# A decoder's state space layer: the skip term as a GpSimd product and a VectorE addition, in place of matmuls with a diagonal

## The chip, the cores and the metric

One NeuronCore of one Trainium2 chip runs the whole kernel in one launch. The metric is device time in microseconds (us), the median of several executions. The engines are TensorE (PE in the rows; PEld is its weight load), VectorE (DVE), ScalarE (ACT), GpSimd (POOL) and SyncE (SP), which here only issues transfers.

## What is computed

The kernel is a two-layer decoder on 32 sequences of 64 tokens, width 256: attention, cross attention and routed experts, then a state space layer, cross attention and low-rank experts, each followed by a residual and a layer norm. The change is in the state space layer (`_L1_attn_ref`):

```python
zxbcdt = u @ W_in.T
z, xBC, dt = jnp.split(zxbcdt, [D_INNER, D_INNER + CONV_DIM], axis=-1)
...
xBC = jax.nn.silu(conv)
x, B, C = jnp.split(xBC, [D_XB, 2 * D_XB], axis=-1)
x = jnp.repeat(x.reshape(b, l, XB_GROUPS, D_STATE), REPEAT, axis=2).reshape(b, l, D_INNER)
...
y = Y_diag + Y_off + xc * D[:, None]
...
y = y * jax.nn.silu(z)
yg = y.reshape(b, l, NGROUPS, NORM_GS)
rstd = jax.lax.rsqrt(jnp.mean(yg * yg, axis=-1, keepdims=True) + EPS)
y = (yg * rstd).reshape(b, l, D_INNER) * norm_weight
return y @ W_out.T
```

The skip term is `xc * D`: the convolved and activated input x, 128 channels that are repeated for 4 groups, times one number per head (8 heads of 64 channels, 512 in all).

## The kernel before

The 2048 tokens are 16 tiles of 128 (two sequences of 64) in 4 chunks of 512. The sequences are so short that the state space recurrence is written as one 64x64 matrix of weights per head and sequence, as in attention.

`layer1_state_space` writes out each engine's program by hand, in 16 slots, one per tile, followed by 7 slots that overlap the cross attention. In slot s the engines do, in this order:

- TensorE: `mix(s)` (L2288), which multiplies the inputs by the weights `es` and leaves the tile's output y in PSUM; `products(s + 1)` (L2273), the products of B and C for the next tile; `square_sums(s - 1)` (L2297); `put_out(s - 2)` (L2307), the output projection. Around them lie, by a table of jobs (`dealt`), the input projections of the chunks to come (`fill`, L2242), transposes (L2248, L2254) and the sums of decays (`segments`, L2261).
- VectorE: `weigh(s)` (L2131) finishes the weights, for which mix(s) waits; `add_up(s - 3)` (L2151, four instructions) adds the projected output to the residual; `gated(s)` (L2142) takes y out of PSUM with the gate silu(z); `statistics(s - 3)` (L2162, L2164) for the layer norm; a convolution (L2113, three instructions); `mean_square(s - 1)` (L2170); often a second convolution; `time(s + 1)` (L2124).
- ScalarE: exponentials of the decays (`decay`, L2030), evacuation of the projections (`evacuate`, L2000 to L2016), squares of the gated output (L2036), activation of the convolved rows (L2024), the layer norm (L2040).
- GpSimd: decay products for later tiles (`decay_steps`, L1922, two in each of slots 0 and 1 of every four), a weight product for tile s + 3 (`weight_steps`, L1928), `rms_power(s - 1)` (L1935), which waits for mean_square(s - 1), and `variance_power(s - 3)` (L1942 to L1948).

The skip term is made by TensorE. Ahead of the slots GpSimd forms `ddiag` (L1958), for each head D times a 64x64 identity, and mix(q) accumulates the product of the inputs with it and the product with the weights in the same PSUM region:

```python
for n, moving in enumerate((ddiag, es[q % 5])):
    ins = pe.matmul(y_ps[a * 64:(a + 1) * 64, b, 0:G * T], xt[c % 2][seq, t, a * 64:(a + 1) * 64],
                    moving[seq, a::2, :], start=(n == 0), stop=(n == 1))
```

This runs for two sequences b and two halves a of the channels, each on its own quarter of the array; an fp32 matmul is two passes in the trace (x8 for four). mix(q) waits for y_out of tile q - 1, because y has one PSUM buffer. The gate then is one instruction on VectorE:

```python
dve.tensor_tensor(yz[q % 4][:].rearrange("p g (b l) -> p b g l", b=2), y, z, ALU.mult).then_inc(y_out, 1)
```

## Time and profile before

| | us |
|---|---|
| median of 3 runs | 1167.17 (1164.1 to 1168.81) |
| profiled execution, its own time | 1169.61 |
| profiled execution, span in the trace | 1167.7 |
| the slots of this layer, first gate to last | 628.7 to 765.5 |
| products with the diagonal in L2288 | 128 passes of 64x256 |
| gate L2142 | 16 of 0.69 |

The span runs from the first to the last instruction that the profiler recorded; the execution's own time has what lies around it. Rows name an operation by line, engine and tile: `cps_o` is the PSUM bank in which y lies, `cps_h` those of the projections, `cps_x` those of the decays, of B and C products and of the square sums, `cps_t` those of the output projection. In windows, the numbers after the length are busy time (and instructions) of PE, PEld, DVE, ACT and POOL, then the granted TensorE clock as a share, the DMA share and GB/s. In timelines a bracket gives the idle time of the engine in front of the instruction and what ended it.

### The profile page before, as it was taken

Reading aid. Unit: us, or ns where it says so; the run is one execution under the profiler, and the core shown is the slowest. Engines: PE = TensorE matmul, PEld = TensorE weight load, DVE = VectorE, ACT = ScalarE, POOL = GpSimd, SP = SyncE. Lnnn points to the kernel's source line nnn. Section 1 sums busy time; section 2 is a strip of 40 time slices with the busy share of each in tenths; the row PEclk is TensorE's granted clock in tenths of the full one; section 3 lists DMA queues with packets and bytes.
Section 4 is the critical chain, followed back from the end, with each engine's and each line's share of the span. In section 5 each row is a group of like instructions: output and inputs, shape, how many; then the busy total and the mean of one; then the engine's idle time right before and its main releaser. Section 6 shows DMA issues by size and latency. Waiting matters only on the chain.

```text
span 1167.7 us, 20743 instructions
## 1 busy us (share of the span) xinstructions
PE 1080.9 (93%) x7208; PEld 652.5 (56%) x7208; DVE 788.3 (68%) x1500; ACT 585.7 (50%) x1212; POOL 491.4 (42%) x868
## 2 busy tenths in 40 slices
PE   6899999999999899999978999889998999999997
PEld 3666675555555345777533455567775435545455
DVE  4999978888887242333586687687997565554655
ACT  2666638777778421333286555367874232121210
POOL 6999854666665255333325254472331000000001
PEclk9999999999999899999989999999999999999999
DMA  6965365665563313453503000120000000000000
GB/s 231 315 193 180 107 188 156 149 155 147 152 152 80 95 68 100 130 173 100 168 4 135 1 1 1 37 82 22 9 24 6 1 0 1 13 5 10 9 10 28
DMA packets 82460, 100.36 MB, mean 86 GB/s; under 512 B 13716, under 2 KB 69166, under 8 KB 81678
## 3 DMA queue, kind: packets, MB, share of 16 engines
q1 hardware_dynamic: 74915, 85.97, 25.8%
q0 software_dynamic: 3408, 9.34, 2.3%
q10 hardware_dynamic: 4034, 3.72, 0.9%
q8 instruction: 60, 0.98, 0.4%
q14 instruction: 43, 0.34, 0.1%
HBM read 59.83 MB, written 33.36 MB: 80 GB/s over the span
## 4 chain that ended last, share of the span: by engine, by line
PE 35%; DVE 5%; ACT 5%; issue 4%; POOL 1%; POOLq 0%; ACTq 0%; DVEq 0%
PE cps_h L3102 6%; PE cps_h L2242 3%; PE cps_h L3121 3%; PE cps_x L3135 2%; PE cps_t L2307 2%; PE cps_h L2733 2%; PE cps_x L3160 2%; PE cps_o L3160 2%; PE cps_t L3121 1%; PE cps_o L3121 1%; ACT e_kbd L2548 1%; PE cps_t L3135 1%; PE cps_x L2664 1%; PE cps_o L2688 1%; PE cps_x L2261 1%
## 5 line engine op out<-in xcount | busy, mean ns | idle before, releaser
L2864 POOL TENSOR_SCALAR f_rstd<-f_mv 128x1 f32<-128x1 f32 x16 | 3.8, 239 | 253.0 <-DVE f_mv L3016 252.9
L932 DVE TENSOR_REDUCE b_nm<-a_s 128x4 f32<-128x1024 f32 x64 | 78.1, 1220 | 33.4 <-PE a_s L1049 32.1
L2961 DVE TENSOR_TENSOR f_prod<-f_sg,f_kept 128x512 f32<-128x512 f32 (+1 forms) x48 | 33.2, 692 | 94.8 <-ACT f_kept L2892 90.9
L996 ACT ACTIVATE a_late<-a_qkv 128x512 f32<-128x512 f32 x128 | 76.3, 596 | 40.0 <-PE a_qkv L1109 39.4
L3102 PE MATMUL cps_h<-residT,w_f_w 128*128 128x512 f32 x176 | 80.8, 598 | 3.4 <-DVE f_inner L2998 1.9
L932 DVE TENSOR_REDUCE b_nm<-a_pt 128x4 f32<-128x1024 f32 x64 | 77.0, 1203 | 2.0 <-PE a_pt L1049 2.0
L996 ACT ACTIVATE a_late<-a_y 128x512 f32<-128x512 f32 x128 | 76.4, 597 | 1.9
L2886 ACT ACTIVATE f_sg<-cps_h 128x512 f32<-128x512 f32 (+1 forms) x24 | 14.3, 596 | 123.6 <-PE cps_h L3121 107.6
L1124 PE MATMUL a_o<-a_late,b_vt 128*32 128x256 f32 x1024 | 68.4, 385 | 5.7 <-ACT a_late L996 5.7
L1441 POOL DMA_INDIRECT routed<-c_out,c_target x39 | 37.4, 959 | 68.8 <-ACT c_out L1523 68.5
L2113 DVE SCALAR_TENSOR_TENSOR d_acc<-d_pad,d_cw,d_acc 128x512 f32<-128x512 f32 x72 | 58.0, 810 | 2.8 <-ACT d_acc L2016 1.1
L351 POOL TENSOR_TENSOR a_nrm<-a_ss,phalf 128x20 f32<-128x20 f32 x16 | 56.9, 3557 | 4.3 <-DVE a_ss L469 4.3
L1649 DVE TENSOR_TENSOR c_hid<-c_sg,cps_h 128x176 f32<-128x176 f32 x39 | 13.2, 338 | 64.7 <-ACT c_sg L1517 64.7
L1711 PE MATMUL cps_h<-c_wgu,c_xT 128*128 x156 | 54.2, 471 | 0.6 <-ACT c_xT L1511 0.6
L3102 PEld LDWEIGHTS cps_h<-residT,w_f_w 128*128 128x128 f32 x176 | 32.5, 190 | 39.1 <-issue 33.1
L1935 POOL TENSOR_TENSOR d_rs<-d_ms,mhalf 128x4 f32<-128x4 f32 x16 | 23.3, 1456 | 64.7 <-DVE d_ms L2170 64.7
L2242 PE MATMUL cps_h<-residT,d_win 128*128 128x512 f32 x96 | 46.7, 618 | 0.8 <-ACT residT L1484 0.5
L1124 PEld LDWEIGHTS a_o<-a_late,b_vt 128*32 128x32 f32 x1024 | 27.7, 109 | 30.2 <-issue 10.9
L2886 ACT ACTIVATE f_sg<-f_kept 128x512 f32<-128x512 f32 (+1 forms) x24 | 15.1, 630 | 58.1 <-DVE f_kept L2966 58.1
L1435 POOL DMA_INDIRECT xrows<-c_xr,c_place_int x32 | 31.0, 967 | 29.0 <-DVE c_xr L1618 19.5
L1730 PE MATMUL cps_o<-c_wd,c_hT 88*128 x156 | 40.1, 380 | 0.0
L3121 PE MATMUL cps_h<-f_inner,w_f_b 128*128 128x512 f32 x80 | 37.6, 593 | 0.0
(448 smaller groups left out, 2906.4 us busy)
## 6 DMA issues: line engine op xcount, KB each, us to landing
kparts<-a_rest SPq DMA_DIRECT2D x48, 192.0 KB, 3.3
a_rest<-a_rest SPq DMA_DIRECT2D x64, 128.0 KB, 3.0
xrows<-in_c_fill SPq DMA_DIRECT2D x13, 387.0 KB, 4.5
c_xrow<-xrows SPq DMA_DIRECT2D x39, 129.0 KB, 2.1
c_back<-routed SPq DMA_DIRECT2D x16, 256.0 KB, 3.3
a_front<-kparts SPq DMA_DIRECT2D x12, 288.0 KB
a_front<-qparts SPq DMA_DIRECT2D x36, 96.0 KB
qparts<-b_xp SPq DMA_DIRECT2D x48, 64.0 KB, 2.9
```

The lines of the kernel that those rows point to most:

```text
L351: gp.tensor_tensor(nrm[v][:], ss[v][:], k.phalf[:, 0:H20], ALU.pow).then_inc(rooted, 1)
L932: dve.tensor_reduce(nm[s % 2][:, 4 * n:4 * n + 4].rearrange("p (g h) -> p g h", h=2), s1[step % 2][:], AX.X, ALU.max, negate=True).then_in ...
L996: act.activation(pr[g % 8][:], s2[g % 2][:], ACT.Exp, scale=SCALE).then_inc(s2_out, 1)
L1124: ins = pe.matmul(o_ps[32 * j:32 * j + 32, q % 2, :], vt[x % 2][:, lh, g, :], pr[g % 8][:, lh, :], start=(lh == 0), stop=(lh == KD - 1))
L1441: gp.indirect_dma_start(routed[:], bass.IndirectOffsetOnAxis(ap=target[s % 8][:], axis=0), out[s % 4][:], None).then_inc(sent[s % 4], 16)
L1711: ins = pe.matmul(h_ps[s % 2][:, 0:2 * F], xT[s % 2][:, kd, :], wgu[:, kd, ds(e, 1), :].rearrange("p a f -> p (a f)"), start=(kd == 0), st ...
L1730: ins = pe.matmul(o_ps[:, s % 2, 0:D], hT[s % 2][:, c, :], wd2[:, ds(e, 1), c, :].rearrange("p a f -> p (a f)"), start=(c == 0), stop=(c = ...
L2113: ins = dve.scalar_tensor_tensor(out=acc[v][:], in0=pad[v][:, :, tap:tap + T], scalar=cw[:, m, tap:tap + 1], in1=acc[v][:], op0=ALU.mult, ...
L2242: ins = pe.matmul(bank[:], win[:, kd, m * P:(m + 1) * P] if m < XT else wz[:, kd, (m - XT) * P:(m - XT + 1) * P], k.residT[:, kd, c * CHUN ...
L3102: pe.matmul(h_ps[j][:], (w1, w3)[j][:, kd, m * P:(m + 1) * P], k.residT[:, kd, c * CHUNK:(c + 1) * CHUNK], start=(kd == 0), stop=False)
L3121: ins = pe.matmul(bank[j][:], b[:, m * P:(m + 1) * P], inner[c % 2][j][choice][:], start=(choice == 1), stop=True)
L3160: pe.matmul(bank[:, 0:D], hid[c % 2][:, m, t * P:(t + 1) * P], w2[:, m, :], start=(m == 0), stop=False)
```

## The change

The diagonal goes. GpSimd makes, for each tile, the product of the convolved inputs with a column of D (`direct_term`, into two buffers `direct`), and VectorE's gate becomes two instructions: y plus the direct term into yz, and yz times the gate in place. TensorE's mix has only the products with the weights, and waits for `y_taken` (the addition) instead of `y_out`.

```diff
+            def direct_term(q):
+                c, t = divmod(q, TPC)
+                if t == 0:
+                    gp.wait_ge(activated, nth["in", c, 0] + 1)
+                if q >= 2:
+                    gp.wait_ge(y_taken, q - 1)
+                x = xc[c % 2][:, t * P:(t + 1) * P].rearrange("p (b l) -> p b l", b=2)
+                gp.tensor_tensor(direct[q % 2][:], x.unsqueeze(2).broadcast_to([P, 2, G, T]),
+                                 dcol[:].unsqueeze(1).unsqueeze(3).broadcast_to([P, 2, G, T]), ALU.mult).then_inc(direct_done, 1)
...
-            gp.tensor_tensor(ddiag[:], dd[:].unsqueeze(2).broadcast_to([P, NH, T]),
-                             eye[:].unsqueeze(1).broadcast_to([P, NH, T]), ALU.mult).then_inc(diag_done, 1)
...
             weight_steps(2)
+            direct_term(0)
+            direct_term(1)
             for s in range(SLOTS):
...
                 if live(s - 3):
                     variance_power(s - 3)
+                if s >= 1 and live(s + 1):
+                    direct_term(s + 1)
...
                 if c >= 2:
                     act.wait_ge(g_full, TPC * (c - 1))
+                    act.wait_ge(direct_done, TPC * (c - 1))
...
-                dve.tensor_tensor(yz[q % 4][:].rearrange("p g (b l) -> p b g l", b=2), y, z, ALU.mult).then_inc(y_out, 1)
+                out = yz[q % 4][:].rearrange("p g (b l) -> p b g l", b=2)
+                dve.wait_ge(direct_done, q + 1)
+                dve.tensor_tensor(out, y, direct[q % 2][:], ALU.add).then_inc(y_taken, 1)
+                dve.wait_ge(y_taken, q + 1)
+                dve.tensor_tensor(out, out, z, ALU.mult).then_inc(y_out, 1)
...
                 if q >= 1:
-                    pe.wait_ge(y_out, q)
+                    pe.wait_ge(y_taken, q)
                 for b in range(2):
                     seq = slice(b * T, (b + 1) * T)
                     for a in range(2):
-                        for n, moving in enumerate((ddiag, es[q % 5])):
-                            ins = pe.matmul(y_ps[a * 64:(a + 1) * 64, b, 0:G * T], xt[c % 2][seq, t, a * 64:(a + 1) * 64],
-                                            moving[seq, a::2, :], start=(n == 0), stop=(n == 1))
+                        ins = pe.matmul(y_ps[a * 64:(a + 1) * 64, b, 0:G * T], xt[c % 2][seq, t, a * 64:(a + 1) * 64],
+                                        es[q % 5][seq, a::2, :], start=True, stop=True)
```

The small arrays for the diagonal (`d_dd`, `d_eye`) are replaced by one (`d_dcol`, 128x4), so one transfer fewer is issued.

Two places of the engines' programs show what moved. The first is the end of a slot on GpSimd, before the change: the root for tile s - 1 (L1935) and the four small steps of the layer norm for tile s - 3.

```order
L1935 TENSOR_TENSOR d_rs<-d_ms,mhalf 128x4
L1942 TENSOR_SCALAR d_rstd<-d_mv 128x1
L1944 TENSOR_TENSOR d_rstd<-d_rstd,mhalf 128x1
L1946 TENSOR_TENSOR d_shift<-d_mv,d_rstd 128x1
L1948 TENSOR_SCALAR d_shift<-d_shift 128x1
```

The same place after the change, with the start of the next slot behind the row of `d_direct`:

```order
L1946 TENSOR_TENSOR d_rs<-d_ms,mhalf 128x4
L1953 TENSOR_SCALAR d_rstd<-d_mv 128x1
L1955 TENSOR_TENSOR d_rstd<-d_rstd,mhalf 128x1
L1957 TENSOR_TENSOR d_shift<-d_mv,d_rstd 128x1
L1959 TENSOR_SCALAR d_shift<-d_shift 128x1
L1939 TENSOR_TENSOR d_direct<-d_xc,d_dcol 128x512
L1923 TENSOR_TENSOR d_dam<-d_dta,d_upto 128x512 x2
L1929 TENSOR_TENSOR d_dtm<-d_dt,d_upto 128x512
```

The product for tile s + 1 (`d_direct`) stands last in slot s, behind the root that waits for mean_square(s - 1); in the slots where decay products are due, as here, three products follow it.

The second place is VectorE in a slot with two convolutions, from the four additions of add_up to the next weighing, after the change (before it, L2142 stood alone in place of the first and second row):

```order
L2158 TENSOR_TENSOR d_yz<-cps_o,d_direct 128x2x4x64
L2160 TENSOR_TENSOR d_yz<-d_yz,d_zs 128x2x4x64
L2180 BN_STATS d_stats<-d_r 128x6
L2182 BN_AGGR d_mv<-d_stats 128x2
L2127 SCALAR_TENSOR_TENSOR d_acc<-d_pad,d_cw,d_acc 128x512 x3
L2188 TENSOR_SCALAR d_ms<-cps_x 128x4
L2127 SCALAR_TENSOR_TENSOR d_acc<-d_pad,d_cw,d_acc 128x512 x3
L2138 TENSOR_TENSOR d_es<-d_es,d_dtm 128x512
L2145 TENSOR_TENSOR d_es<-d_es,cps_x 128x512
```

The mean square stands behind both gate instructions, so what waits for it on GpSimd waits for both.

## Rows read from the trace of the kernel before

**Rows 1.** The page: busy time of each engine, its share of the span, and instructions.
```profile
PE 1080.9 (93%) x7208; PEld 652.5 (56%) x7208; DVE 788.3 (68%) x1500; ACT 585.7 (50%) x1212; POOL 491.4 (42%) x868
```

**Rows 2.** Windows of slots 10 and 13 (start:end length, busy by engine, clock, DMA).
```profile
731.80:738.00 6.20, 6.18 (x50) 4.32 (x50) 5.49 (x13) 1.67 (x4) 3.72 (x7) 1.00 0.57 172
...
754.10:759.00 4.90, 4.90 (x43) 3.63 (x42) 4.56 (x11) 1.12 (x2) 2.63 (x5) 1.00 0.00 0
```

**Rows 3.** Waits in the stage, 627 to 766 us: total, times, longest.
```profile
DVE d_yz L2142 <- PE cps_o L2288: 25.8, 9, 6.5
...
PEld cps_o L2288 <- DVE d_es L2131: 8.6, 9, 2.7
```

**Rows 4.** The chain of waits, slots 5 and 6: start us, us, piece.
```profile
682.36 0.69 DVE d_yz L2142
...
688.75 0.70 DVE d_es L2131
...
689.49 1.12 PE cps_o L2288 x16
```

**Rows 5.** Timeline of TensorE: start us, us, line, tile, count, wait before and releaser.
```profile
661.97 1.10 PE L2261 MATMUL cps_x<-d_dam,d_later 128*128 128x512 f32 x2 [1.29 <-ACT d_es L2030]
...
712.25 0.68 PE L2288 MATMUL cps_o<-d_ddiag,d_xt 64*64 64x256 f32 x8
...
713.30 0.65 PE L2273 MATMUL cps_x<-d_cT,d_bT 128*64 128x256 f32 x4
713.88 1.98 PE L2242 MATMUL cps_h<-residT,d_wz 128*128 128x512 f32 x4
```

**Rows 6.** Timeline of GpSimd ahead of the stage.
```profile
596.46 1.04 POOL L1958 TENSOR_TENSOR d_ddiag<-d_dd,d_eye 128x512 f32<-128x512 f32 x1
606.33 0.24 POOL L1961 TENSOR_SCALAR d_an<-d_an 128x8 f32<-128x8 f32 x1 [8.84 <-ACT d_an L2061]
```

**Rows 7.** Timeline of VectorE, slots 1, 5, 7 and 9.
```profile
640.95 0.16 DVE L2170 TENSOR_SCALAR d_ms<-cps_x 128x4 f32<-128x4 f32 x1 [0.30 <-PE cps_x L2297]
...
682.36 0.69 DVE L2142 TENSOR_TENSOR d_yz<-cps_o,d_zs 128x512 f32<-128x512 f32 x1 [0.37 <-PE cps_o L2288]
682.97 0.42 DVE L2162 BATCH_NORM_STATS2 d_stats<-d_r 128x6 f32<-128x256 f32 x1
...
688.03 0.68 DVE L2124 TENSOR_TENSOR d_es<-d_es,d_dtm 128x512 f32<-128x512 f32 x1
688.75 0.69 DVE L2131 TENSOR_TENSOR d_es<-d_es,cps_x 128x512 f32<-128x512 f32 x1
...
702.31 0.69 DVE L2142 TENSOR_TENSOR d_yz<-cps_o,d_zs 128x512 f32<-128x512 f32 x1 [5.78 <-PE cps_o L2288]
...
724.69 0.69 DVE L2142 TENSOR_TENSOR d_yz<-cps_o,d_zs 128x512 f32<-128x512 f32 x1 [2.01 <-PE cps_o L2288]
```

**Rows 8.** Timelines of VectorE and GpSimd, 613 to 619 us.
```profile
612.84 5.18 DVE L2113 SCALAR_TENSOR_TENSOR d_acc<-d_pad,d_cw,d_acc 128x512 f32<-128x512 f32 x4
617.93 1.52 DVE L2124 TENSOR_TENSOR d_es<-d_es,d_dtm 128x512 f32<-128x512 f32 x1
...
614.52 1.49 POOL L1928 TENSOR_TENSOR d_dtm<-d_dt,d_upto 128x512 f32<-128x512 f32 x1
```

**Rows 9.** Timelines of VectorE and GpSimd in the tail, slots 12 to 15.
```profile
752.37 0.16 DVE L2170 TENSOR_SCALAR d_ms<-cps_x 128x4 f32<-128x4 f32 x1 [0.26 <-PE cps_x L2297]
...
756.22 0.68 DVE L2142 TENSOR_TENSOR d_yz<-cps_o,d_zs 128x512 f32<-128x512 f32 x1
...
757.37 0.14 DVE L2170 TENSOR_SCALAR d_ms<-cps_x 128x4 f32<-128x4 f32 x1
...
765.55 0.68 DVE L2142 TENSOR_TENSOR d_yz<-cps_o,d_zs 128x512 f32<-128x512 f32 x1
...
755.37 0.23 POOL L1948 TENSOR_SCALAR d_shift<-d_shift 128x1 f32<-128x1 f32 x1
```

**Rows 10.** Timeline of TensorE: the cross attention's first product.
```profile
768.88 1.16 PE L2664 MATMUL cps_x<-residT,w_e_wq 128*128 128x128 f32 x8 [1.20 <-DVE w_e_wo L2645]
```

More of the change, by code:

```diff
@@ L1856, in layer1_state_space @@
         wdt, cw, cb = sb("wdt", [P, KD, 32]), sb("cw", [P, XT, CW]), sb("cb", [P, XT])
-        bias, alog, dd = sb("bias", [P, NH]), sb("alog", [P, NH]), sb("dd", [P, NH])
-        later, upto, eye = sb("later", [P, P]), sb("upto", [P, T]), sb("eye", [P, T])
+        bias, alog = sb("bias", [P, NH]), sb("alog", [P, NH])
+        later, upto, dcol = sb("later", [P, P]), sb("upto", [P, T]), sb("dcol", [P, G])
         q_, p_ = (sb(n, [P, TILES, NH]) for n in ("q", "p"))
-        an, ddiag, acc = sb("an", [P, NH]), sb("ddiag", [P, NH, T]), many(4, "acc", [P, SPC, T])
+        an, acc, direct = sb("an", [P, NH]), many(4, "acc", [P, SPC, T]), many(2, "direct", [P, 2, G, T])
         bT, cT = many(2, "bT", [P, CHUNK]), many(2, "cT", [P, G, CHUNK])
@@ L1875, in layer1_state_space @@
         conv_consts = ((win, io["d_win"][:, :, 0:XT * P]), (cw, io["d_cw"]), (cb, io["d_cb"]))
-        consts = ((upto, "d_upto"), (later, "d_later"), (dd, "d_dd"), (eye, "d_eye"), (wout, "d_wout"), (nw, "d_nw"))
+        consts = ((upto, "d_upto"), (later, "d_later"), (dcol, "d_dcol"), (wout, "d_wout"), (nw, "d_nw"))
         conv_const, gate_const = sem("d_conv_const_in"), sem("d_gate_const_in")
@@ L1879, in layer1_state_space @@
         dt_full, pre, ab_done, e_done, an_exp = sem("d_dt_full"), sem("d_pre_steps"), sem("d_ab_done"), sem("d_e_done"), sem("d_an_exp")
-        an_done, dt_done, wout_done, diag_done, padded = sem("d_an_done"), sem("d_dt_done"), sem("d_wout_done"), sem("d_diag_done"), sem("d_padded")
+        an_done, dt_done, wout_done, direct_done, padded = sem("d_an_done"), sem("d_dt_done"), sem("d_wout_done"), sem("d_direct_done"), sem("d_padded")
         dta_done, timed = sem("d_dta_done"), sem("d_timed")
@@ L1884, in layer1_state_space @@
         g_full, w_done = sem("d_g_full"), sem("d_w_done")
+        y_taken = sem("d_y_taken")
         y_full, y_out, sq_done, ss_full, ms_out, rs_done = (sem("d_" + n) for n in ("y_full", "y_out", "sq_done", "ss_full", "ms_out", "rs_done"))
@@ L1905, in between @@
                 elif s in (18, 20, 22):
-                    for dst, src in consts[s - 18:s - 16]:
+                    for dst, src in (consts[0:2], consts[2:4], consts[4:])[(s - 18) // 2]:
                         sp.dma_start(dst[:], io[src]).then_inc(const, 16)
@@ L2278, in mix @@
                 pe.wait_ge(w_done, q + 1)
-                pe.wait_ge(diag_done, 1)
                 if t == 0:
@@ L3358, in state_space_layout @@
     out["d_cb"] = f["L1_attn_conv_b"].reshape(-1, P).T
-    for name, src in (("d_bias", "dt_bias"), ("d_alog", "A_log"), ("d_dd", "D")):
+    for name, src in (("d_bias", "dt_bias"), ("d_alog", "A_log")):
         out[name] = np.tile(f["L1_attn_" + src][None], (P, 1))
+    out["d_dcol"] = np.repeat(f["L1_attn_D"].reshape(G, 2).T, P // 2, axis=0)
     row = np.arange(P)
@@ L3364, in state_space_layout @@
     out["d_upto"] = (row[:, None] % T <= np.arange(T)[None, :]).astype(np.float32)
-    out["d_eye"] = (row[:, None] % T == np.arange(T)[None, :]).astype(np.float32)
 def cross_layout(f, out, rows_to_parts, order):
```

## The prediction, made before the result was known

> **What bounds the kernel now.** I read the page first: TensorE is busy 93% of the span, VectorE 68%, GpSimd 42% [rows 1]. That average says that time taken from TensorE is worth something and that GpSimd has room. The change touches one stage, the state space layer (some 627 to 769 us), so the windows of that stage come next. In slot 10 (731.8 to 738.0) TensorE is busy 6.18 of 6.20 us and VectorE 5.49, in slot 13 (754.1 to 759.0) TensorE 4.90 and VectorE 4.56 of 4.90 [rows 2]: the reader is to see that neither engine has much room, and at the stage's end VectorE almost none. The list of waits over the stage shows both: VectorE waits for the mixing products (L2288) 25.8 us in 9 of 16 slots, and the weight loads of those products wait for the weighing on VectorE (L2131) 8.6 us in 9 [rows 3]. The chain of waits alternates: in slot 5 it enters VectorE at the gate (682.36), leaves it at the weighing (688.75) and goes back to TensorE for the mixing of slot 6 [rows 4]. So the cost of a VectorE instruction has to be read slot by slot.
>
> **What is removed.** Eight of sixteen matmul passes per tile. With sixteen, the mixing holds TensorE from 712.25 to 713.30, 1.05 us. The nearest thing to the mixing afterwards is the group behind it, L2273: two sequences, two passes each of 256 columns, next group 0.58 us later [rows 5]. After the change each of four array quarters gets two passes of 256 columns. I take 0.58: 0.47 less per tile. The bounds are 0 (the passes of the four quarters overlap, so fewer need not be shorter) and 0.52 (half). The product that made the diagonal (1.04 us at 596.46) and one small transfer also go. GpSimd waits 8.8 us behind that product [rows 6], so they cost nothing either way.
>
> **What is added on VectorE.** One instruction per tile. The gate takes 0.69 us; the addition has its form (PSUM and SBUF in), and the multiplication that of L2124 (two SBUF operands, 0.68). A dependent instruction follows 0.72 us behind the start of the one before (688.03, 688.75), the next independent one starts 0.61 us behind the gate (682.36, 682.97) [rows 7]. So each tile costs 0.72 us more. TensorE's next mixing waits only for the addition, which comes when the gate came.
>
> **Collisions.** The multiplication, unlike the gate, reads SBUF twice. At 617.93 such a product took 1.52 us instead of 0.68 while GpSimd made its products, four convolution steps took 5.18, and one of GpSimd's 1.49 instead of 1.04 [rows 6, 8]. I charge 0.70 per collision, a little under the 0.84 of that row because the overlap need not be whole (bounds 0 and 1.04, one whole GpSimd product). Where? GpSimd's work in a slot ends with the new product; in slots 4, 5, 8 and 9 two decay products and one weight product follow, 3.1 us, and they move from beside the additions (L2151, one SBUF input) to beside the multiplication. In slot 1 the new product meets the convolution and L2124.
> The Trainium skill, SBUF — State Buffer, section "Who interferes with whom", says that a VectorE instruction with two SBUF inputs contends with a GpSimd instruction that reads SBUF, and that the loser blocks for the whole instruction. The trace agrees on who collides; by its rule each collision could cost a whole GpSimd product, which would make the sum 4 x 0.34 = 1.4 us larger.
>
> **The sum, slot by slot**, as the shift of the next mixing.
> - Slots 0 and 1 run over VectorE, with the new work: 2 x (0.72 - 0.47) = 0.5, less 0.3 us that the mean square of slot 1 waits for TensorE at 640.95 [rows 7] and no longer would, plus one collision: +0.9.
> - Slots 2, 6, 8 and 10 are TensorE's: VectorE's work disappears in its waits (5.8 us in front of the gate of slot 7 [rows 7]). -0.47 each: -1.9.
> - Slots 3, 7 and 11: TensorE waits for the exponentials of ScalarE, 1.3 us in slot 3 [rows 5], and less work ahead of a wait only makes it longer. 0.
> - Slots 4 and 5: VectorE. Two multiplications with two collisions, 2 x 1.42, less the 0.37 us that it waited [rows 7]: +2.5.
> - Slot 9: the gate's wait of 2.0 us [rows 7] absorbs slot 8's; then VectorE decides up to the mixing of slot 10, 1.42: +1.4.
> - Slots 12 to 15 and the way out: +4.3, below.
> Together 0.9 - 1.9 + 2.5 + 1.4 + 4.3 = **+7.2 us**.
>
> **The tail.** From slot 12 there is no convolution, and the gate comes every 4.7 us (756.22, then 765.55 two slots on) [rows 9]. In the new order GpSimd has a loop there: the mean square on VectorE (L2170) releases the root (L1935), four small steps follow, then the product for the next tile, for which the next gate waits, behind which stands the next mean square. Its length: gate to mean square 1.15 us (756.22 to 757.37) plus 0.72; mean square to the end of the small steps 3.24 (752.37 to 755.37 + 0.23) [rows 9]; the product 1.04 with 0.06 of signalling. 6.2 us against 4.7. Gate 13 comes 0.5 late (the mean square at 752.37 stays where it is, since the gate in front comes 0.47 earlier and takes 0.72 more; 752.4 + 3.24 + 1.1 = 756.7), 14 and 15 each 1.55 later, and the last multiplication adds 0.72: 4.3. That moves in full to the cross attention, whose first product on TensorE stands waiting for VectorE, 1.2 us [rows 10].
> Queued behind the new wait on VectorE are the layer norm statistics, the mean square and the next weighing; behind GpSimd's own wait, for the addition of two slots ago, nothing is late.
>
> The profiled execution took 1169.61 us (span 1167.7), 2.4 above the median of 1167.17. 1169.6 + 7.2 = 1176.8 in its terms; 1167.2 + 7.2 = **1174.4** at the median.
>
> **The rivals.**
> - *TensorE gets its time back.* VectorE's 25.8 us of waiting [rows 3] absorb both instructions everywhere, and 16 x 0.47 = 7.5 go: 1159.7. For it: 93% busy [rows 1]. Against it: the chain passes along VectorE in slot 5 [rows 4], and in the tail there is no wait in front of the gate.
> - *No collisions.* GpSimd's products slip past the multiplications, which are 0.7 us long: 7.2 - 4 x 0.7 = 4.4, 1171.6. For it: the products pass within a microsecond of the multiplications, and my times for both are no better than that.
> - *Dearer.* The new product takes the 1.49 us of a contended one [rows 8] in the tail (3 x 0.45, +1.4), and the collisions cost 1.04 (+1.4), with two more of 0.7 where products now meet the convolution (+1.4): 1174.4 + 4.2 = 1178.6. TensorE idles more in the tail, but its granted clock is 1.00 in slots 10 and 13 [rows 2], the full 2.4 GHz, and its wait of 1.3 us in slot 3 [rows 5] lies in a stage that kept 1.00 too; I charge nothing for it.
> - *The mixing gets no shorter.* Half the passes, same time: the 0.47 of TensorE's four slots and of the first two go missing, 2.8: 1177.2. For it: the passes of different quarters overlap already.
> A rule that speaks against the change: the Trainium skill, GPSIMD Engine Reference, section "Engine selection", gives elementwise products to VectorE, GpSimd being about twice as slow. Here it is 1.04 against 0.68 [rows 6, 7]. It is the loop of the tail that this ratio makes long.
>
> **How the numbers follow.** A difference of 0.5%, 5.8 us, is about what a measurement can tell. My sum has chance 0.40, with some 3 us either way; TensorE's gain 0.13, no collisions 0.22, dearer 0.20, no shorter mixing 0.05. The range reaches from halfway to the first rival to past the dearer one: 1163 to 1180. Faster by over 0.5% (under 1161.3) holds most of the first rival: 0.10. Within it (to 1173.0): a third of my sum, two thirds of no collisions, some of the first: 0.36. Slower: 0.54.
>
> **What would show it.** The profile after should have: mixing groups of 0.58 us; 16 GpSimd products of about 1.04 us and 16 multiplications, four or five of them near 1.4; gates 13 to 15 waiting for GpSimd's product and 6.2 us apart; TensorE waiting longer for the weighing. From gate 13 to the cross attention's first product (756.22 to 768.88) it is 12.7 us now and some 16.5 then. It is wrong if the gates in the tail stay under 5.4 us apart, or if slots 4, 5 and 9 grow by less than 0.5 us each.

## The result and the profile after

The changed kernel takes **1187.76 us** in the median of 4 runs (1183.24 to 1188.78) against 1167.99 of the kernel before (4 runs, 1164.10 to 1174.62): a ratio of 1.0138, 95% interval [1.0092, 1.0184]. The forecast was 1174.4 with a range up to 1180, so the direction was right and the size was not: +19.8 between the medians where +7.2 was expected. The ratio on record is not the quotient of the two medians (that is 1.0169); taken as the measure it says +16.1 us, between 10.7 and 21.5. Two later sets of runs gave 1.0137 [1.0105, 1.0169] and 1.0147 [1.0089, 1.0206].

The page of after, busy time of each engine, its share of the span and instructions (profiled execution: 1188.27 us, span 1186.2, against 1169.61 and 1167.7):

```profile
PE 1086.4 (92%) x7080; PEld 651.5 (55%) x7080; DVE 802.2 (68%) x1516; ACT 586.2 (49%) x1212; POOL 509.6 (43%) x883
```

Beside [rows 1]: TensorE has 128 matmuls fewer (16 tiles by 8) and is yet busy 5.5 us longer, VectorE has 16 instructions and 13.9 us more, GpSimd 15 and 18.2. The second number of TensorE is where to look. The whole stage, from the first mixing to the cross attention's first product, as one window (start:end, length, busy by engine, granted clock of TensorE, DMA), of before and then of after:

```profile
627.40:768.80 141.40, 130.50 (x717) 74.49 (x716) 105.07 (x200) 72.08 (x122) 64.81 (x86) 1.00 0.09 29
```

```profile
628.40:787.20 158.80, 136.59 (x589) 75.45 (x589) 120.90 (x216) 72.18 (x122) 80.40 (x100) 0.91 0.07 26
```

The stage grew by 17.4 us, nearly all of the 18.5 by which the span grew. VectorE's 15.8 and GpSimd's 15.6 us more are for the most part the new instructions. The column nobody had charged for is the granted clock: 1.00 before (the full 2.4 GHz), 0.91 after. It is 27.3 us at 1.2 GHz in six stretches; outside the stage the two traces have nearly the same, 31.2 and 31.6 us.

**What was forecast of the order came out.** TensorE in slots 4 to 6 and at three places behind (start us, us, line, tile, count, wait before and releaser):

```profile
676.20 0.66 PE L2304 MATMUL cps_o<-d_es,d_xt 64*64 64x256 f32 x8
676.79 0.65 PE L2291 MATMUL cps_x<-d_cT,d_bT 128*64 128x256 f32 x4
...
686.19 0.66 PE L2304 MATMUL cps_o<-d_es,d_xt 64*64 64x256 f32 x8 [0.78 <-DVE d_es L2145]
...
696.69 0.73 PE L2304 MATMUL cps_o<-d_es,d_xt 64*64 64x256 f32 x8 [3.00 <-DVE d_es L2145]
697.34 1.12 PE L2291 MATMUL cps_x<-d_cT,d_bT 128*64 128x256 f32 x4
...
700.87 3.51 PE L2323 MATMUL cps_t<-d_wout,d_yz 128*128 128x256 f32 x8
...
751.28 1.57 PE L2279 MATMUL cps_x<-d_dam,d_later 128*128 128x512 f32 x2 [2.24 <-ACT d_es L2044]
...
780.31 0.66 PE L2304 MATMUL cps_o<-d_es,d_xt 64*64 64x256 f32 x8 [2.20 <-DVE d_es L2145]
```

The mixing takes 0.59 us to the next group (676.20 to 676.79) instead of 1.05. In slot 6 TensorE waits 3.00 us for the weighing where before it had waited 0.40, behind the weighing at 688.75 [rows 4]:

```profile
689.49 0.69 PE L2288 MATMUL cps_o<-d_ddiag,d_xt 64*64 64x256 f32 x8 [0.40 <-DVE d_es L2131]
```

And in after, right behind that wait the group that takes 0.65 us at 676.79 takes 1.12 at 697.34; the output product takes 3.51 us (1.97 in slot 4). The same three slots as windows show it in one column:

```profile
675.80:686.20 10.40, 9.62 (x44) 5.03 (x43) 10.05 (x18) 6.57 (x11) 7.80 (x9) 1.00 0.01 2
686.20:696.70 10.50, 7.50 (x38) 4.26 (x39) 10.15 (x18) 4.54 (x9) 7.89 (x9) 1.00 0.00 1
696.70:705.00 8.30, 8.30 (x34) 6.04 (x35) 5.54 (x13) 0.84 (x2) 5.61 (x9) 0.59 0.00 0
```

In the second TensorE is busy 7.50 of 10.50 us, VectorE 10.15; in the third TensorE is busy all the time, at a clock of 0.59.

VectorE's gates and multiplications of tiles 4, 5, 8, 14 and 15:

```profile
677.49 0.68 DVE L2158 TENSOR_TENSOR d_yz<-cps_o,d_direct 128x512 f32<-128x512 f32 x1
678.20 1.28 DVE L2160 TENSOR_TENSOR d_yz<-d_yz,d_zs 128x512 f32<-128x512 f32 x1
...
688.72 1.27 DVE L2160 TENSOR_TENSOR d_yz<-d_yz,d_zs 128x512 f32<-128x512 f32 x1
...
724.23 1.27 DVE L2160 TENSOR_TENSOR d_yz<-d_yz,d_zs 128x512 f32<-128x512 f32 x1
...
776.87 0.69 DVE L2158 TENSOR_TENSOR d_yz<-cps_o,d_direct 128x512 f32<-128x512 f32 x1 [0.92 <-POOL d_direct L1939]
...
783.13 0.69 DVE L2158 TENSOR_TENSOR d_yz<-cps_o,d_direct 128x512 f32<-128x512 f32 x1 [0.92 <-POOL d_direct L1939]
```

The addition stands where the gate stood, the multiplication 0.71 us behind. Four multiplications, of tiles 4, 5, 8 and 9, take 1.26 to 1.28 us, the others 0.69. GpSimd beside the one of tile 5:

```profile
687.39 2.04 POOL L1923 TENSOR_TENSOR d_dam<-d_dta,d_upto 128x512 f32<-128x512 f32 x2
689.39 1.49 POOL L1929 TENSOR_TENSOR d_dtm<-d_dt,d_upto 128x512 f32<-128x512 f32 x1
```

The multiplication starts at 688.72, 0.71 us ahead of the end of the decay products (687.39 + 2.04), and loses 0.58. The weight product starts at 689.39, 0.60 ahead of the end of the multiplication, and loses 0.45 (1.49 for 1.04). So the later of the two loses about what is left of the earlier one. In the tail the gates of tiles 14 and 15 wait for GpSimd's product and come 6.26 us apart; the forecast said 6.2, from 4.7 [rows 9]. The gate of tile 13 (770.62) has no such wait here, and that of tile 11 (750.76) has one of 0.92 that was not forecast. From gate 13 to the cross attention's first product it is 16.6 us, forecast some 16.5.

The ledger of the sum, slot by slot: what the distance between two mixings has gained on the kernel before. The last columns are the same changed kernel in a second trace, and an experiment told below in which its waits are covered:

| slots | forecast | after | after again | waits covered |
|---|---|---|---|---|
| 0, 1 | +0.9 | 0.40, 2.12 | 0.40, 0.74 | 0.40, 0.74 |
| 2 | -0.47 | -0.46 | -0.46 | -0.47 |
| 3 | 0 | 1.66 | 0.00 | 0.81 |
| 4, 5 | +2.5 | 0.40, 2.15 | 0.41, 2.15 | 0.49, 2.08 |
| 6 | -0.47 | 2.78 | 2.83 | -0.45 |
| 7 | 0 | 0.00 | 0.01 | 0.00 |
| 8 | -0.47 | -0.45 | -0.46 | -0.45 |
| 9 | +1.4 | 1.35 | 1.35 | 1.35 |
| 10 | -0.47 | -0.46 | -0.46 | -0.45 |
| 11 | 0 | 1.36 | 1.37 | 1.17 |
| 12 to 15 | +4.3 | 6.54 | 6.38 | 4.36 |
| sum | +7.2 | +17.4 | +14.3 | +9.6 |

Every entry without a stretch at half clock is within 0.25 us of its forecast, but for slots 3 and 11 of the last column, where the filler itself was too long (below). The ones that are off (1, 3, 6, 11, and 12 to 15) are those with a stretch in them: 27.3 us in all in after, 20.5 in the second trace. What a stretch costs depends on the slot: 3.4 us at half clock cost 1.4 us in slot 1 and 1.7 in slot 3, 6.8 us cost 3.2 in slot 6, and slot 15, where the last chain runs over VectorE, grew by 1.45 us in after and in its second trace, with 3.4 us at half clock in it, and by 1.45 with its waits covered and none.

### The profile page after: what moved, and what is told of

It reads as the page before. It is cut to its first block, busy times and chain, and to the rows that moved or that the text cites. A ratio compares the mean times of both kernels' runs of the same rounds, so it can differ in the third digit from the quotient of the medians.

```text
span 1186.2 us, 20518 instructions
## 1 busy us (share of the span) xinstructions
PE 1086.4 (92%) x7080; PEld 651.5 (55%) x7080; DVE 802.2 (68%) x1516; ACT 586.2 (49%) x1212; POOL 509.6 (43%) x883
## 4 chain that ended last, share of the span: by engine, by line
PE 44%; DVE 8%; ACT 5%; issue 5%; POOL 4%; DMA 0%; POOLq 0%; ACTq 0%; DVEq 0%; SPq 0%
PE cps_h L3118 7%; PE cps_h L1711 4%; PE cps_o L1730 3%; PE cps_h L3137 3%; POOL xrows L1435 3%; PE cps_h L2260 2%; DVE d_acc L2127 2%; PE cps_x L3151 2%; PE cps_h L2749 2%; PE cps_t L2323 1%; PE cps_x L3176 1%; PE cps_o L3176 1%; PE cps_t L3137 1%; PE cps_o L3137 1%; ACT e_kbd L2564 1%
## 5 line engine op out<-in xcount | busy, mean ns | idle before, releaser
L2902 ACT ACTIVATE f_sg<-cps_h 128x512 f32<-128x512 f32 (+1 forms) x24 | 14.3, 596 | 125.3 <-PE cps_h L3137 109.3
```

## The experiments

**Theory**: VectorE's second instruction and GpSimd's loop cost what was forecast, and by opening waits on TensorE they bring its clock down, which costs as much again. **Rivals**: the mechanisms of the order cost more than the sum said; or the clock falls for another reason, TensorE's lighter load after losing its passes, or the chance of one execution. Each kernel is compared with the kernel before on the same chip; chips differ (1170 us on some, 1184 on others).

**The same kernels again.** Is the half clock the program's or the execution's?

> The changed kernel, unchanged, on the same chip. A and B: 16 to 20 us over the kernel before, the stage 157 to 160 us with 20 to 30 us at half clock. If it is below +10 here, the falls are a matter of the execution and not of the program.

> The kernel before, unchanged, so that the others have its trace from their own chip. The stage (first mixing product to the cross attention's first product) 141 to 143 us, with at most one fall of the granted clock in it (A and B).

> The changed kernel a third time. A: 20 to 27 us at half clock in the stage as in the two traces before, 16 to 19 us over the kernel before. If the half clock is under 10 us here, its count is a matter of the single execution and the other runs' counts decide nothing.

Measured: 1186.75, 1169.86 (ratio 0.9985 [0.9956, 1.0014]) and 1187.53 us. At half clock in the stage: 20.5, 0 and 27.2 us. The stage took 155.7, 141.4 and 158.3 us. So it is the program's in the main, and the single execution's in the detail: the stretches of slots 1 and 3 come and go. The first two traces of after differ by 3.1 us in the stage for 6.8 us of half clock. The traced execution of the first of these sets was the shortest of its six (1177.97 us): it had only 21.0 us at half clock outside the stage, where the kernel before had 44.9 in its trace from this chip. So the counts of one trace are to be read with care; further down they are compared with those of all executions.

### One part at a time

**The gate in two steps alone**, on the kernel before (`direct` a buffer of zeros):

```diff
-                dve.tensor_tensor(yz[q % 4][:].rearrange("p g (b l) -> p b g l", b=2), y, z, ALU.mult).then_inc(y_out, 1)
+                dve.tensor_tensor(out, y, direct[:], ALU.add).then_inc(y_taken, 1)
+                dve.wait_ge(y_taken, q + 1)
+                dve.tensor_tensor(out, out, z, ALU.mult).then_inc(y_out, 1)
...
-                    pe.wait_ge(y_out, q)
+                    pe.wait_ge(y_taken, q)
```

> The kernel before with its diagonal product, and the gate in two VectorE instructions: it adds a buffer of zeros and then multiplies, TensorE released by the addition. GpSimd makes no products per tile. It is VectorE's price alone. My ledger without the 0.47 of TensorE: slots 0 and 1 +1.1, 4 and 5 +1.1 (and collisions of at most 2 x 0.7), slot 9 +0.7, slots 12 to 15 +2.9, together +5.8 to +7.2: 1173 to 1175. A: no falls of the clock. B: longer waits bring falls, 1178 or more.

Measured: 1193.61 against 1183.87 us, ratio 1.0080 [1.0064, 1.0097]. The stage took 150.6 us, of which 3.3 are in slot 6, the slot with its one stretch at half clock (6.8 us, behind a wait of 2.30); the other slots add up to 5.9. The 5.9 hold two collisions: the multiplications of tiles 4 and 5 take 1.28 and 1.27 us here too, beside the products that GpSimd makes in the kernel before. VectorE's instruction is the largest part of what was added, and it alone opens the wait of slot 6.

**GpSimd's product alone**, made beside the kernel before and not used:

```diff
+                if s >= 1 and live(s + 1):
+                    gp.wait_ge(direct_done, s + 1)
+                    direct_term(s + 1)
```

> The kernel before, with the changed kernel's GpSimd products made and not used (one buffer, so each waits for the one before). GpSimd's part alone. Nothing waits for them on VectorE; they shift the decay and weight products by 1.04 us and meet two-operand instructions of VectorE in slots 1 to 3, 8 and 9. My ledger: one collision that counts in slot 1 (0.7), some overlap with the convolutions: +0.5 to +2.5. A: no falls of the clock, since TensorE has its passes. B: none either, the waits being short.

Measured: 1174.10 against 1169.94 us, ratio 1.0034 [1.0014, 1.0054]. The stage took 146.4 us: 0.9 more in slot 1, 1.0 in slot 5, and 3.1 in slot 11, where a stretch of 6.8 us at half clock follows a wait of 1.79. The kernel before has the same wait (at 740.86 in its trace) and no stretch behind it. VectorE in slot 4 of this kernel:

```profile
671.09 3.08 DVE L2132 SCALAR_TENSOR_TENSOR d_acc<-d_pad,d_cw,d_acc 128x512 f32<-128x512 f32 x3
...
674.16 2.32 DVE L2132 SCALAR_TENSOR_TENSOR d_acc<-d_pad,d_cw,d_acc 128x512 f32<-128x512 f32 x3
```

and GpSimd beside it:

```profile
671.33 1.50 POOL L1929 TENSOR_TENSOR d_dtm<-d_dt,d_upto 128x512 f32<-128x512 f32 x1
```

The first convolution meets GpSimd's weight product, which the new product has pushed back, and takes 0.76 us more than the second, which meets nothing. In slot 5 it is the same (3.07 us, in the kernel before 2.29), and there it is in the way of the next mixing.

**The passes alone**: the kernel before without the diagonal's eight passes. This leaves the skip term out of the computation.

```diff
-                        for n, moving in enumerate((ddiag, es[q % 5])):
-                            ins = pe.matmul(y_ps[a * 64:(a + 1) * 64, b, 0:G * T], xt[c % 2][seq, t, a * 64:(a + 1) * 64],
-                                            moving[seq, a::2, :], start=(n == 0), stop=(n == 1))
+                        ins = pe.matmul(y_ps[a * 64:(a + 1) * 64, b, 0:G * T], xt[c % 2][seq, t, a * 64:(a + 1) * 64],
+                                        es[q % 5][seq, a::2, :], start=True, stop=True)
```

> The kernel before without the product with the diagonal (the skip term is left out), VectorE and GpSimd as before. It is the gain side of the change alone. My ledger: 0.47 us in each slot that TensorE or its round trip with VectorE decides, 10 or 11 of them, so -5 us: 1162. Theory A: fewer passes bring falls of the clock in the stage even with the old waits, each 1.7 us or so: 1163 to 1170. Theory B: no new falls, 1160 to 1163.

Measured: 1183.13 against 1183.87 us, ratio 0.9990 [0.9955, 1.0024]. The stage took 141.8 us, no less than before. Its slots 0 to 10 and 13 to 15 give back 3.8 us, and slots 11 and 12 take 4.2 more, with 10.2 us at half clock behind waits of 2.24 and 1.78 us. Eight passes fewer per tile bring no gain that can be told even where nothing is added for them (the interval leaves room for up to 0.45%, 5 us). In the trace the reason is that the gain is turned into waits, and two of the waits are followed by the lower clock.

**The passes back**, in the changed kernel: the mixing issued twice.

```diff
+                        for n in range(2):
+                            ins = pe.matmul(y_ps[a * 64:(a + 1) * 64, b, 0:G * T], xt[c % 2][seq, t, a * 64:(a + 1) * 64],
+                                            es[q % 5][seq, a::2, :], start=True, stop=True)
```

> The changed kernel with each of its mixing products issued twice (the second overwrites the first with the same numbers), so TensorE has its sixteen passes per tile again, and VectorE and GpSimd are as changed. Theory A: some 10 of the 18.5 us are the granted clock, which falls in six places of the stage because TensorE lost half of its mixing passes while it waits longer. Then the falls are gone or nearly (at most 1 or 2 in the stage), mixing takes 1.05 us again, which costs up to 6 x 0.47 = 2.8 us, and the time is 1176 to 1181, less than the changed kernel's 1188 although it does more. Theory B: the falls come from the longer waits for VectorE and GpSimd alone. Then they stay, and the time is 1188 to 1191.

Measured: 1198.29 against 1183.87 us, ratio 1.0129 [1.0098, 1.0160]; stage 154.0, of it 9.0 at half clock. The trace has less than after by 1.7 to 4.8 us in the stage though TensorE does more. But in time the kernel is no faster than the changed one (1.0138), and over its four executions it has as much half clock (table below). So TensorE's old load did not bring the clock back: the gain that theory A gave for it did not come.

**The loop of the tail taken away**: GpSimd's product for the next tile ahead of the root and the small steps.

```diff
+                if s >= 1 and live(s + 1):
+                    direct_term(s + 1)
                 if live(s - 1):
                     rms_power(s - 1)
                 if live(s - 3):
                     variance_power(s - 3)
-                if s >= 1 and live(s + 1):
-                    direct_term(s + 1)
```

> The changed kernel with GpSimd's product for tile s + 1 put ahead of the root and the small steps of slot s. Both theories: the loop over GpSimd in slots 13 to 15 is gone (gates 5.3 us apart there instead of 6.3, none waiting for GpSimd), 3 to 4 us. A: with shorter waits one or two falls in the tail go too, 1180 to 1185. B: the same falls elsewhere, 1180 to 1185; the run tells the loop's price, not A from B.

Measured: 1194.30 against 1183.87 us, ratio 1.0084 [1.0047, 1.0121]; stage 156.2, at half clock 27.3 us as in after, so 2.6 less with the same amount of half clock. The gates of tiles 12, 13 and 14 on VectorE:

```profile
778.58 0.69 DVE L2158 TENSOR_TENSOR d_yz<-cps_o,d_direct 128x512 f32<-128x512 f32 x1 [1.80 <-ACT residT L2013]
...
783.97 0.68 DVE L2158 TENSOR_TENSOR d_yz<-cps_o,d_direct 128x512 f32<-128x512 f32 x1
...
789.22 0.68 DVE L2158 TENSOR_TENSOR d_yz<-cps_o,d_direct 128x512 f32<-128x512 f32 x1
```

5.39 and 5.25 us apart (and 5.25 to that of tile 15) and no wait for GpSimd, where after had 6.26: the loop was there, and it was GpSimd's.

**Both together**, the passes back and the product first:

> The changed kernel with its mixing products issued twice, behind the wait, and GpSimd's product ahead of the root. A and B: 3 to 4 us less than with the passes back alone, which was 14.4 over the kernel before: 10 to 12. Against the filler ahead of the wait it tells what eight passes cost when they lie on the round trip weigh, mix, gate: 8 to 10 slots x 0.47, 3 to 4 us more than there.

Measured: 1183.34 against 1170.88 us, ratio 1.0098 [1.0070, 1.0126]; stage 153.5, at half clock 10.2 us. Against the passes back alone (1.0129) that is the 3 to 4 us expected; against the filler with the product first (1.0093, below) the expected 3 to 4 us more do not show.

### Does work on TensorE keep the clock up?

**Filler per tile**: in the changed kernel eight passes whose result is overwritten, ahead of the wait for the weights.

```diff
+                for moving in (wout[:, 0, :], None):
+                    if moving is None:
+                        pe.wait_ge(w_done, q + 1)
...
```

> The changed kernel with eight filler passes per tile in front of TensorE's wait for the weights: products of the inputs with a constant, which the real products then overwrite. TensorE has sixteen passes per tile again, and half of them lie in its wait for VectorE. What the experiments so far leave of the two theories. A: little TensorE work and long waits together make the clock fall (20 to 27 us at half clock in the stage with both, 7 to 10 with either alone, 0 in the kernel before). Then here 0 to 10 us at half clock, and the time is that of my ledger: +7.2, plus 4 x 0.47 in TensorE's slots, plus up to 4 for the falls left: 9 to 13 us over the kernel before, where the changed kernel has 17. B: waits alone: still 20 us at half clock, 17 to 20 us over the kernel before.

> The same with GpSimd's product ahead of the root and the small steps. A: 3.6 us less than with the filler alone, 5 to 9 us over the kernel before, at most 10 us at half clock in the stage. B: 13 us or more.

Measured: 1181.32 us, ratio 1.0114 [1.0071, 1.0157], stage 153.1, half clock 10.2 us; and with the product first 1185.41 us, ratio 1.0093 [1.0056, 1.0131], stage 155.6, half clock 20.5. The second contradicts what was expected of it: filler under every tile and 20.5 us all the same. TensorE in slot 6 there:

```profile
688.76 0.66 PE L2308 MATMUL cps_o<-d_wout,d_xt 64*64 64x256 f32 x8
691.84 1.13 PE L2308 MATMUL cps_o<-d_es,d_xt 64*64 64x256 f32 x8 [2.41 <-DVE d_es L2145]
692.90 1.12 PE L2291 MATMUL cps_x<-d_cT,d_bT 128*64 128x256 f32 x4
```

The filler is over in 0.5 us, and a wait of 2.41 is left, at whose end the clock is down. It was spread evenly where the waits are not, so the theory in that form (as much work as before, and the clock holds) does not fit this trace. The executions of this kernel fall into two groups, four at 1172 to 1178 us and six at 1185 to 1190; the traced one is of the upper group. Counted over each whole execution, the four have 28 to 38 us at half clock and the six 47 to 71.

**The diagonal's passes ahead of the wait**, in the kernel before, to shorten its own waits:

```diff
+                for n, moving in enumerate((ddiag, es[q % 5])):
+                    if n == 1:
+                        pe.wait_ge(w_done, q + 1)
...
```

> The kernel before, with the four products with the diagonal moved in front of TensorE's wait for the weights. The work is the same; the diagonal's passes lie in TensorE's wait where it waits for VectorE (9 mixings, 8.6 us in all), which shortens the round trip weigh, mix, gate by up to 0.47 us in slots 1, 6, 10 and the tail. A: 2 to 4 us less than before, no fall of the clock in the stage. B: the same. If the mixing's end comes no sooner, the passes of one array quarter do not care for the order, and the time is the same.

Measured: 1168.57 against 1169.94 us, ratio 0.9975 [0.9948, 1.0001]: perhaps a quarter of a per cent, and not settled. Its stage took 142.7 us, with one stretch of 6.8 us in slot 12, behind a wait of 1.78 which the kernel before has too. That slot grew by 3.2 us; the others together gave back 2.0, the least that was expected.

### The waits themselves

The traces of the stage were then read in one more way: each wait of TensorE of 1 us or more, and whether a stretch at half clock begins next to its end (from 0.7 us ahead of it to 2.6 behind). All 20 traces of this study together, those of the six runs that follow included:

| wait of TensorE, us | waits | followed by half clock |
|---|---|---|
| 1.0 to 1.5 | 38 | 3 |
| 1.5 to 2.0 | 48 | 16 |
| 2.0 to 2.5 | 25 | 14 |
| 2.5 to 3.0 | 6 | 4 |
| 3.0 and more | 7 | 7 |

None of the 44 stretches begins elsewhere. The kernel before has no wait over 1.83 us; after has five of 2.2 to 3.0, four of them followed. A count is no cause, so six runs followed, three pairs.

**The waits covered**, in the changed kernel: overwritten passes only where TensorE waited, as long as it waited (tiles 1, 2, 6, 10, 15; behind the mixing of tiles 3 and 11; slot 12), and the same **with the product first** (there 2 groups and not 4 at tile 15):

```diff
+                cover_y(q, {1: 4, 2: 1, 6: 5, 10: 4, 15: 4}.get(q, 0))
+                pe.wait_ge(w_done, q + 1)
...
+                if s in (3, 11):
+                    pe.wait_ge(ms_out, s - 1)
+                    for _ in range({3: 6, 11: 8}[s]):
+                        pe.matmul(g_ps[:, 0:G * T], later[:], wout[:, 0, :], start=True, stop=True)
```

> The changed kernel, with TensorE given matmuls whose results are overwritten (output weights as moving data) in the places where it waited over 1.1 us in the trace of after: ahead of the mixing of tiles 1, 2, 6, 10 and 15 (4, 1, 5, 4 and 4 groups of 8 passes, 0.48 us each), behind the mixing of tiles 3 and 11 (6 and 8 passes of 0.25 us), and ahead of the transposes of slot 12 (3 groups). They end before the data come, so they should delay nothing. Theory, falls follow waits: in the 14 traces of the stage so far each stretch at half clock begins at the end of a TensorE wait of over 1.1 us, and the longer the wait the likelier it is (2 of 29 waits of 1.0 to 1.5 us, 12 of 38 of 1.5 to 2.0, 20 of 31 above). With no wait over 0.8 us left there: half clock in the stage under 7 us, stage 147 to 151 us, 8 to 11 us over the kernel before. Rival, the falls come from the lower load of the whole stage or by chance: eight places of filler change little, 20 us and more at half clock, 15 us and more over before.

> As the covered waits, and GpSimd's product for the next tile ahead of the root and the small steps, which takes away the loop of the tail. Theory, falls follow waits: half clock under 7 us, stage 144 to 148 us, 4 to 8 us over the kernel before, what is left being the slots that run over VectorE. Rival: as the product first alone, 10 us and more over.

Measured: 1195.47 against 1184.77 us, ratio 1.0073 [1.0047, 1.0100]; and 1193.16 us, ratio 1.0068 [1.0045, 1.0090]. The stage took 151.0 and 147.5 us, and neither has any half clock ahead of its last 0.2 us. Just there a stretch begins in both, behind the wait of the cross attention's first product (2.94 and 1.93 us). The window of the whole stage of the first:

```profile
642.60:793.60 151.00, 139.72 (x785) 79.63 (x784) 120.64 (x216) 72.21 (x122) 81.43 (x101) 1.00 0.08 28
```

More work for TensorE than in after (139.7 us busy against 136.6), 7.8 us less time. In slot 3 the filler was too long:

```profile
676.04 2.86 PE L2386 MATMUL cps_x<-d_wout,d_later 128*128 128x256 f32 x12
678.73 1.02 PE L2279 MATMUL cps_x<-d_dam,d_later 128*128 128x512 f32 x2
```

2.69 us in a wait of 1.75, and 16 passes of 3.56 us in slot 11 in one of 2.24. That is the 0.8 and the 1.2 of the ledger's last column; without them the stage would have grown by 7.6 us. Time, too, says that the clock was worth more than a third: +10.7 us here, +16.7 to +19.8 in the three sets of after.

**The other way round**: the kernel before with such waits opened, by unused products on VectorE ahead of the weighing, and then with the waits covered by the diagonal's passes made again, VectorE's delay left as it is:

```diff
+                for n in range({1: 1, 6: 4, 10: 3, 15: 3}.get(q, 0)):
+                    dve.wait_ge(spared, before_this[q] + n)
+                    dve.tensor_scalar(spare[:], ddiag[:], 1.0, None, ALU.mult).then_inc(spared, 1)
```

and for the covered one of each pair, on TensorE:

```diff
+                for _ in range({1: 4, 6: 5, 10: 4, 15: 3}.get(q, 0)):
...
+                            pe.matmul(y_ps[a * 64:(a + 1) * 64, b, 0:G * T], xt[c % 2][seq, t, a * 64:(a + 1) * 64],
+                                      ddiag[seq, a::2, :], start=True, stop=True)
+                pe.wait_ge(w_done, q + 1)
```

> The kernel before, all its work and its order, with idle time made for TensorE at four places: VectorE makes 1, 4, 3 and 3 products of 0.72 us whose results are unused ahead of the weighing of tiles 1, 6, 10 and 15. TensorE's waits there should be 2.5, 3.3, 2.5 and 1.5 to 2.2 us, about those of after. The work itself delays by 0.7 + 2.9 + 2.2 + 2.2 at most, 6 to 8 us. Theory, falls follow waits: 10 to 20 us at half clock in the stage and so 4 to 8 us more: 11 to 16 us over the kernel before. Rival, the falls of after come from its shorter mixing or from chance, not from waits: 0 to 7 us at half clock, 6 to 9 us over before, the same as with the waits covered.

> As the waits opened, with TensorE making the diagonal's products again (4, 5, 4 and 3 groups of 8 passes, 0.48 us each) while it would wait ahead of the mixing of tiles 1, 6, 10 and 15. VectorE's delay is the same. Theory, falls follow waits: half clock 0 to 7 us, 6 to 9 us over the kernel before, 4 to 8 us less than with the waits open. Rival: the same time as with the waits open, within 2 us.

Measured: 1191.89 and 1192.72 against 1184.77 us, ratios 1.0046 [1.0016, 1.0075] and 1.0043 [1.0015, 1.0070]. The same time: the rival's number. But the waits had come out short, 2.04, 2.00, 1.54 and 1.09 us, and behind the first three nothing followed; the 10.2 us at half clock lie behind the fourth and behind one that the kernel before has too (1.79). Covered, the stage had none. This pair tells little, except that a wait of 2.0 us alone need not bring the clock down. So it was made again with 3, 6, 5 and 6 products, and 6, 6, 5 and 6 groups to cover:

> The kernel before with longer idle time for TensorE than in the run with waits opened, where 2.0 us had come out and no fall followed at those places: 3, 6, 5 and 6 unused products of 0.72 us on VectorE ahead of the weighing of tiles 1, 6, 10 and 15. TensorE's waits there by the waits of that run: 3.4, 3.4, 3.0 and 3.2 us. Theory, falls follow waits of such length: at least three of the four places followed by half clock, 13 to 30 us in the stage, and 4 to 9 us longer than the same kernel with the waits covered. Rival, it is not the wait but what else is in the changed kernel: at most 7 us at half clock, both times within 2 us.

> The same with TensorE making the diagonal's products again for 6, 6, 5 and 6 groups (0.48 us each) while it would wait. VectorE's delay is the same, some 14 us of work of which the stage should show 9 to 13. Theory: 0 to 7 us at half clock in the stage, 4 to 9 us shorter than with the waits open. Rival: the same time within 2 us.

Measured: **1204.10** and **1196.86** against 1184.42 us, ratios 1.0167 [1.0128, 1.0206] and 1.0088 [1.0057, 1.0119]. The waits were 3.69, 3.63, 3.17 and 2.47 us, and behind all four the clock fell. TensorE in slot 6 with the wait open:

```profile
706.67 1.06 PE L2296 MATMUL cps_o<-d_ddiag,d_xt 64*64 64x256 f32 x8 [3.63 <-DVE d_es L2139]
707.44 1.14 PE L2296 MATMUL cps_o<-d_es,d_xt 64*64 64x256 f32 x8
708.52 1.12 PE L2281 MATMUL cps_x<-d_cT,d_bT 128*64 128x256 f32 x4
```

and covered, where VectorE comes just as late:

```profile
704.49 2.82 PE L2295 MATMUL cps_o<-d_ddiag,d_xt 64*64 64x256 f32 x48
708.20 0.69 PE L2302 MATMUL cps_o<-d_ddiag,d_xt 64*64 64x256 f32 x8 [0.89 <-DVE d_es L2139]
708.68 0.64 PE L2302 MATMUL cps_o<-d_es,d_xt 64*64 64x256 f32 x8
709.25 0.65 PE L2281 MATMUL cps_x<-d_cT,d_bT 128*64 128x256 f32 x4
```

The last row of each is the same group: 1.12 us and 0.65. The windows of the two stages, the first with the waits open:

```profile
638.10:799.90 161.80, 141.81 (x717) 81.66 (x717) 115.06 (x219) 72.03 (x122) 67.31 (x88) 0.92 0.07 26
```

```profile
641.00:795.80 154.80, 143.96 (x901) 83.29 (x900) 115.08 (x220) 71.99 (x122) 66.27 (x86) 0.98 0.08 27
```

24.8 us at half clock against 6.8, and 7.0 us of stage; 7.2 us in the medians. VectorE's busy time is the same.

Does one trace stand for its kernel? The granted clock of every execution is on record, and as the clock is either full or half, 2 x (1 - clock) x span is its time at half clock, of the whole kernel and not of the stage. The means, with the kernel before on the same chip:

| kernel | executions | at half clock, us | before |
|---|---|---|---|
| after, the two sets above | 6, 4 | 52.8, 68.2 | 34.6, 32.7 |
| passes back | 4 | 63.5 | 42.2 |
| waits covered | 11 | 49.0 | 45.8 |
| the same, product first | 12 | 49.2 | 45.8 |
| waits opened | 12 | 51.2 | 45.8 |
| opened and covered | 12 | 49.8 | 45.8 |
| longer waits opened | 6 | 63.7 | 49.2 |
| longer waits covered | 10 | 46.8 | 49.2 |

The waits covered take away nearly all that the changed kernel had too much, and the longer waits bring 14.5 us, which their covering takes away again. The first pair is alike (51.2 and 49.8), as its times are; its one trace with 10.2 us was not typical. In this program the wait is what brings the clock down, and idle time filled with useless work is faster than idle time.

## Why the prediction was wrong

- **Direction and mechanisms: right.** The mixing went from 1.05 to 0.59 us (forecast 0.58), GpSimd's product takes 1.04, the four collisions are in slots 4, 5, 8 and 9, the tail's gates 6.26 us apart (6.2), and TensorE's slots 2, 8 and 10 gave back 0.46 each, slot 6 where its wait was covered. Without half clock (waits covered, slots 3 and 11 taken as 0) the sum is 7.6 us where it said 7.2; slot 11 never ran undisturbed in the changed kernel, and is at most 1.2.
- **Collisions: a little dear, and partly made up by luck.** A contended multiplication took 0.58 us more (1.27 against 0.69), not 0.70. But the first convolution behind it also lost some (2.56 and 2.55 us in slots 4 and 5, before 2.41 and 2.29), which the sum left out; so those slots came to 2.55, forecast 2.5. The Trainium skill, SBUF — State Buffer, section "Who interferes with whom", calls the shared port pair an exclusive lock, and says of VectorE's two-port modes that the engine that comes second is fully blocked. The trace agrees if the price is what is left of the instruction that came first: 0.71 us left, 0.58 lost. The whole 1.04 of the prediction's upper bound would need both to start together.
- **Slot 1: forecast too cheap.** Slots 0 and 1 took 1.14 us, forecast 0.9. The product alone costs 0.9 in slot 1 (product made and not used), where 0.7 had been charged; with the product first that slot grew by -0.14.
- **The step that failed** is in the rival "Dearer": "TensorE idles more in the tail, but its granted clock is 1.00 in slots 10 and 13 [rows 2], the full 2.4 GHz, and its wait of 1.3 us in slot 3 [rows 5] lies in a stage that kept 1.00 too; I charge nothing for it." The rows showed the clock for waits of up to 1.3 us (1.83 in the whole stage) and were used for waits of 2.2 to 3.0 us, which the sum itself created: it had TensorE waiting longer for the weighing, and of slots 3, 7 and 11 it said that less work ahead of a wait "only makes it longer" and priced that at 0. In after, slot 3 grew by 1.66 us, behind a wait of 1.75. So the term put at nothing is the clock behind the longer waits. What that costs is 17.4 - 7.6 = 9.8 us in the trace of after, 0.36 us per us at half clock; 0.33 in the second trace of after, 0.39 in the pair with longer waits. With 10 us for the clock, a number known only afterwards, the forecast would have been 1184.4.
- **The rivals.** "TensorE gets its time back" fell: even with nothing added, the passes taken away give no gain that can be told (ratio 0.9990 [0.9955, 1.0024]). "No collisions" and "the mixing gets no shorter" did not happen. "Dearer" had the right side but the wrong reasons: in the tail the new product took 1.04, not 1.49 us.
- The Trainium skill, GPSIMD Engine Reference, section "Engine selection", gives elementwise products to VectorE. Its reason, that GpSimd is about twice as slow, is 1.04 against 0.68 us here. The product's place in GpSimd's order cost 3.6 us: in the stages without half clock, 151.02 us against 147.45 with the product first; 2.9 of it are the loop of the tail and 0.9 slot 1, and slots 4 and 5 took 0.2 back. It is the smaller part of the loss: VectorE's own second instruction cost 5.9.
- **What stays open.** Which waits of 1.5 to 2.5 us are followed by half clock (30 of 73 were): the same wait of the same program went either way from one execution to the next. The covered waits differ from the open ones both in idle time and in TensorE's work there; that work spread over all tiles did not do the same (1.0114), but the two are not fully separated. And no version here beats the kernel before; with the waits covered and the product first it is still 1.0068 [1.0045, 1.0090].

## What to carry to other kernels

When a change takes work from the busiest engine and puts it on one that it waits for, list the waits that this opens on TensorE: where they are longer than any that the trace before has, its clock of 1.00 says nothing of them, and here four to six stretches of 3 to 10 us at half clock cost 7 to 10 us of stage, about as much as all that was added (7.6). Before giving a saved matmul pass a value, see which slots TensorE alone bounds; here it was four of sixteen. And a loop of VectorE and GpSimd over tiles is priced by its length against the distance of the tiles, not by the busy share of either.

## What was not expected of the hardware

- Useless matmuls in a wait of TensorE made the kernel faster: with 3.1 us more of busy time in the stage it took 7.8 us less, and the pair of runs that differ only in such matmuls is 1204.10 against 1196.86 us.
- The lower clock is one of two levels (1.2 GHz against 2.4), and it hits the work behind the wait, while the wait itself is at 1.00 in the window (686.2 to 696.7): a slow matmul group is to be read together with the wait in front of it.
- The clock is not the same in every execution of one program: the kernel before took 1159.55 to 1173.64 us in ten executions on one chip, and two traces of after have 27.3 and 20.5 us at half clock in the stage, with all slots without it alike to 0.05 us.
